# A two-layer graph network on one core: VectorE's work per supertile of the sort reduced or moved, node stages with two buffers, the first table split inside the gather pass

## The reference

```python
def reference(x, src, dst, edge_attr_4, W, ...):       # 12500 nodes, 412500 edges sorted by dst, D = 64
    h = relu(layernorm(x));  x = x + layer0(h, (src, dst), W)
    h = relu(layernorm(x));  x = x + layer1(h, (src, dst), edge_attr_4, ...)
    return x
def layer0(input, edge, weight):                        # hyperbolic attention
    h = mobius_matvec(weight, input, C)
    dist = sqdist(h[edge[0]], h[edge[1]], C)
    edge_e = exp(-leaky_relu(logmap0(C / (C + dist)), 0.2))
    h_prime = segment_sum(edge_e * logmap0(h)[edge[1]], edge[0])
    out = elu(h_prime / segment_sum(edge_e, edge[0]))
    return proj(expmap0(out, C), C)
def layer1(h, edge, edge_attr, ...):                    # message passing, four batch norms
    m = bn_relu(concat(h[src], h[dst], edge_attr) @ Wm1 + bm1)
    m = bn_relu(m @ Wm2 + bm2)
    u = bn_relu(concat(h, segment_sum(m, src)) @ Wu1 + bu1)
    return bn_relu(u @ Wu2 + bu2)
```

## Time and profile before

| what | value |
|---|---|
| median of 3 runs | 17072.78 us (17068.78 to 17084.48) |
| profiled execution, its own time | 17093.01 us |
| its span | 17091.3 us |
| busy: PE | 6354.3 us (37%) |
| busy: DVE | 8652.0 us (51%) |
| busy: ACT | 4054.6 us (24%) |
| busy: POOL | 9635.6 us (56%) |

### The profile page before, as it was taken

How to read it: one execution, slowest core, us unless ns; L and a number is a source line. 1 busy time by engine, 2 the same in 40 slices (tenths; PEclk the granted TensorE clock), 3 DMA queues, 4 the chain that set the end, 5 groups by cost and what they waited for, 6 DMA issues and landing times. The chain is left out here.

```text
span 17091.3 us, 195568 instructions
## 1 busy us (share of the span) xinstructions
PE 6354.3 (37%) x50077; PEld 5035.1 (29%) x50078; DVE 8652.0 (51%) x18303; ACT 4054.6 (24%) x7861; POOL 9635.6 (56%) x9968
## 2 busy tenths in 40 slices
PE   2444444311111111111159522323223223258996
PEld 2444444300000000000058511111111111125995
DVE  5888888623333333333268733333333333346884
ACT  1666666400000000000058400000000000024333
POOL 0555555466656665666657356666666666622773
PEclk7777777655555555555579756655655656579998
DMA  2000000133323332323444222222222222275331
GB/s 58 8 8 8 8 8 8 27 75 75 75 66 73 75 74 68 74 69 74 67 106 151 67 66 66 68 63 68 67 65 68 65 66 68 65 145 187 106 107 54
DMA packets 1142331, 1160.59 MB, mean 68 GB/s; under 512 B 688769, under 2 KB 832769, under 8 KB 1142018
## 3 DMA queue, kind: packets, MB, share of 16 engines
q1 hardware_dynamic: 845634, 680.39, 13.9%
q0 software_dynamic: 235008, 248.13, 8.6%
q10 hardware_dynamic: 61632, 231.44, 3.4%
HBM read 872.56 MB, written 286.75 MB: 68 GB/s over the span
## 5 line engine op out<-in xcount | busy, mean ns | idle before, releaser
L1559 POOL DMA_INDIRECT big<-b_d,big x3424 | 3284.0, 959 | 2270.7 <-POOLq L144 1232.2
L1084 POOL DMA_INDIRECT big<-h_d,big x3424 | 3273.9, 956 | 2001.9 <-issue 1189.0
L1145 DVE TENSOR_REDUCE ps<-ps 128x260 f32<-128x780 f32 x856 | 837.8, 979 | 3275.1 <-remote 1441.1
L1126 PE MATMUL ps<-big 128*128 x3424 | 737.9, 373 | 4609.0 <-issue 3388.5
L1686 DVE TENSOR_REDUCE ps<-ps 128x256 f32<-128x768 f32 x856 | 827.6, 967 | 2582.9 <-DVEq L144 1605.9
L1126 PEld LDWEIGHTS ps<-big 128*128 128x128 bf16 x3424 | 442.4, 162 | 4904.3 <-issue 4901.1
L1638 PE MATMUL ps<-big 128*128 x3424 | 608.7, 335 | 2615.9 <-issue 2130.1
L1885 POOL TENSOR_SCALAR big<-iota_f,big 128x128 f32<-128x128 f32 x1498 | 880.4, 608 | 827.7 <-DMA big<-rec_d 528.3
L1638 PEld LDWEIGHTS ps<-big 128*128 128x128 bf16 x3424 | 444.6, 160 | 2973.7 <-issue 2973.7
L777 ACT ACTIVATE big<-big 128x512 bf16<-128x512 bf16 x1736 | 1076.7, 708 | 907.1 <-ACTq L144 907.1
L1092 ACT ACTIVATE big<-big 128x16 int32<-128x16 f32 x214 | 49.1, 229 | 4899.9 <-issue 2304.5
(11 more groups left out here) (409 smaller groups left out, 14488.7 us busy)
## 6 DMA issues: line engine op xcount, KB each, us to landing
big<-e_d SPq DMA_DIRECT2D x428, 512.0 KB, 3.1
rows_d<-big ACTq DMA_DIRECT2D x214, 544.0 KB
big<-rows_d SPq DMA_DIRECT2D x214, 544.0 KB, 3.2
HA<-slots_d SPq DMA_DIRECT2D x214, 512.0 KB
big<-slots_d SPq DMA_DIRECT2D x214, 512.0 KB
e_d<-big ACTq DMA_DIRECT2D x214, 512.0 KB
big<-rec_d SPq DMA_DIRECT2D x860, 64.0 KB, 2.9
big<-h_d,big POOLq DMA_INDIRECT x3424
```

Of the source, the lines that this page charges most:

```text
L1084: gp.indirect_dma_start(G[g][:, t * ROW:(t + 1) * ROW], None, h0_d, bass.IndirectOffsetOnAxis(idx[g % 2][:, t:t + 1], 0)).then_inc(gath[g] ...
L1126: m = t.matmul(XS[q % 2][:, n, 0:3 * D + 3], OT3[g % 2][:, o, :], T0[:, ds(chunks[o // 2] * TW, 3 * D + 3)], start=True, stop=True)
L1145: v.tensor_reduce(xrow[:, q * QT:(q + 1) * QT, :], XS[q % 2][:, :, 0:3 * D + 3].rearrange("p t (q w) -> p t w q", q=3), AX, ALU.add).then_ ...
L1559: gp.indirect_dma_start(G[g][:, t * D:(t + 1) * D], None, b_d, bass.IndirectOffsetOnAxis(idx[g % 2][:, t:t + 1], 0)).then_inc(gath[g], 16)
```

## The change

**Blanks and edges.** `blank` gets a place of its own at the end of `big` and is set in the starting block; the fill of `rec_d` moves from the sort into SP's queue of the first node stage, which awaits it at its end; the weights for `wblk` go ahead of the edges.

```diff
             def _(sp):
+                sp.wait_ge(s_w, 1)
+                for h in range(2):
+                    sp.dma_start(wblk[h * D:(h + 1) * D, h * D:(h + 1) * D], w0t).then_inc(s_st, 16)
                 for t_, a_ in ((s_i, src), (d_i, dst)):
                     sp.dma_start(t_[0:P - 1, :], a_[0:(P - 1) * COLS].rearrange("(p j) -> p j", p=P - 1)).then_inc(s_edges, 16)
                     sp.dma_start(t_[P - 1:P, 0:LASTE], a_[(P - 1) * COLS:E].rearrange("(p j) -> p j", p=1)).then_inc(s_edges, 16)
-                sp.wait_ge(s_w, 1)
-                for h in range(2):
-                    sp.dma_start(wblk[h * D:(h + 1) * D, h * D:(h + 1) * D], w0t).then_inc(s_st, 16)
+                sp.dma_start(rec_d.rearrange("(k p t) w -> p k (t w)", p=P, t=TB),
+                             blank.unsqueeze(1).to_broadcast([P, NBLK + 2, TB * REC])).then_inc(s_blank, 16)
...
                 sp.wait_ge(s_v, 82)
                 sp.dma_start(h0_d.rearrange("(c p) w -> p c w", p=P), ROWS).then_inc(s_st, 16)
                 sp.wait_ge(s_st, 48)
                 sp.wait_ge(s_edges, 64)
+                sp.wait_ge(s_blank, 32)
```

**Node stages with two buffers.** In the first node stage, in layer 1's and in the final blocks the loops are unrolled; `hT`, `uT`, `stage` and, but for two cases, the PSUM areas exist twice; the node stages transpose straight from `HB` without a copy; PE puts the transpositions of round i+1 ahead of the product of round i. The first one's PE program (the others are alike):

```diff
                 t.wait_ge(s_st, 32)
-                with t.Fori(0, NIT) as i:
-                    hold(t, "t", g_in, i + 1)
+                t.wait_ge(s_v, 14)
+
+                def turn(i):
+                    if i >= 2:
+                        t.wait_ge(g_cp, i - 1)
...
+                turn(0)
+                for i in range(NIT):
+                    if i + 1 < NIT:
+                        turn(i + 1)
+                    product(i)
```

In layer 1's, ACT copies the second product from PSUM to `AG` and each round is stored on its own:

```diff
-                    link(v.tensor_copy(SB3, PAB[:, :, D:2 * D]))
-                    link(v.tensor_copy(AG[:, ds(i * W, W)], SB))
...
+                    a.activation(AG[:, i * W:(i + 1) * W].rearrange("p (c d) -> p c d", d=D), PAB[:, :, D:2 * D], ACT.Copy
+                                 ).then_inc(g_b, 1)
```

In the final blocks the PSUM areas alternate in the second and third (`h = i % 2 * 2048`) and stay single in the first. The addition of `AG` and `AG2`, one instruction ahead of the loop before, is made round by round, `bn_stats` follow round by round (`chunk_stats`), and the output is stored in 7 pieces and the last rows:

```diff
+        def chunk_stats(v, link, Y, i):
+
+            done = lambda n: min(n * W // NS5, 25)
+            for n in range(done(i), done(i + 1)):
+                ins = v.bn_stats(nst[:, n * 6:(n + 1) * 6], Y[:, n * NS5:(n + 1) * NS5])
...
+                concat(0)
+                concat(1)
                 link, k = chain(v, s_v)
-                node_stats(v, link, Y1, mv1, colp[:, 2:3], colp[:, 4:5], sc1, sh1, s_a, 1)
+                for i in range(NIT):
+                    if i + 2 < NIT:
+                        concat(i + 2)
+                    v.wait_ge(f_y, i + 1)
+                    chunk_stats(v, link, Y1, i)
+                node_stats(v, link, mv1, colp[:, 2:3], colp[:, 4:5], sc1, sh1, s_a, 1)
...
+                for i in range(NIT):
+                    sp.wait_ge(f_add, i + 1)
+                    c0, c1 = i * CPI, min((i + 1) * CPI, NCH - 1)
+                    sp.dma_start(out[c0 * P:c1 * P, :].rearrange("(c p) d -> p c d", p=P), X[:, c0:c1, :]).then_inc(s_out, 16)
```

```diff
-                        last = t.matmul(joint2, HI[b][:, m:NHI * w:step], LO[b][:, m:NLO * w:step], start=(n == 0 and m == 0),
+                        last = t.matmul(joint2, LO[b][:, m:NLO * w:step], HI[b][:, m:NHI * w:step], start=(n == 0 and m == 0),
```

```diff
-        ACTD = 14
+        ACTD = 16
...
-                    need(go(v.tensor_tensor(hit3, INC.unsqueeze(1).to_broadcast([P, NW, NC + 1]),
-                                            g8.unsqueeze(2).to_broadcast([P, NW, NC + 1]), ALU.is_le)))
-                    need(go(v.tensor_tensor(hit3, hit3, STEP.unsqueeze(1).to_broadcast([P, NW, NC + 1]), ALU.mult)))
-                    need(go(v.tensor_reduce(dsum, hit3, AX, ALU.add)))
+                    for w in range(NW):
+                        n = go(v.scalar_tensor_tensor(out=hit3[:, w, :], in0=INC, scalar=g8[:, w:w + 1], in1=STEP,
+                                                      op0=ALU.is_le, op1=ALU.mult, accum_out=dsum[:, w:w + 1]))
+                    need(n)
...
+                def attributes(b):
+
+                    consume(gp, att_in[b], 32)
+                    a3 = attb[b].rearrange("p (j a) -> p j a", a=4)
+                    r3 = rem.rearrange("p (j a) -> p j a", a=4)
+                    gp.tensor_copy(PA[b][:, :, 0, :], a3).then_inc(s_piece, 1)
+                    gp.wait_ge(s_piece, 1)
+                    gp.tensor_tensor(r3, a3, PA[b][:, :, 0, :], ALU.subtract).then_inc(s_piece, 1)
...
                 def spread(b, s):
+                    attributes(b)
                     consume(gp, l_rdy)
-                    consume(gp, pa_rdy)
```

```diff
+                sp.dma_start(R0, h0_d.rearrange("(c p) w -> p c w", p=P)).then_inc(s_table, 16)
...
+                t.wait_ge(t0_rdy, 1)
                 each_block(t, step)
...
+                v.wait_ge(s_table, 16)
+                piece3(v, split, R0[:, :, 0:D], R0t, T0q)
+                piece3(v, split, R0[:, :, SQ:SQ + 1], q2t, T2q)
+                v.sem_inc(t0_rdy, 1)
```

363 lines of the change are left out of this document (198 added, 165 removed).

## The result

| | before | after |
|---|---|---|
| median of 4 runs each | 17070.78 us | 16429.32 us |
| lowest and highest | 17068.22 to 17084.48 | 16424.54 to 16432.72 |
| span of the profiled execution | 17091.3 us | 16422.8 us |

The ratio is 0.9622 (95% interval 0.9606 to 0.9639): 641 us or 3.8% less.

What follows compares the result with a forecast made beforehand. Each stage between barriers has its own limit, DVE in the supertiles; 76 + 8 + 295 + 40 + 3 + 72 + 100 = 594 us off the profiled 17093.0 gives 16499, as a median 16480, range 16370 to 16640.

Steps and rivals of the forecast that it cites:

- First node stage: Node stage before the sort: weights first start PE 78 us sooner; stage ends at 212, saving 76 us, bounds 60 and 100.
- Histogram: Sort's histogram with swapped operands: gain up to 38 us or loss of 15 possible, costed at nothing.
- Wait for the casts: DVE's wait for `s_cast` before the first `flags` in the sort goes: 8 us saved.
- Supertiles: Sort's supertiles: DVE saves 3.0 us each, period falls from 23.2 to 20.8, 295 us saved; bounds 370 and 135.
- the second loop: Supertiles' chain through POOL's `spread` and PE's `place` and `ranks`: 20.6 us, 20.8 with a hand-over, becomes the bound.
- the rival to which I gave 0.15: Supertiles: chain over POOL and PE is shorter, or histogram gains clock; period 20.2, 75 us better, 16405; chance 0.15.
- POOL and DVE hinder each other: Supertiles: POOL's new instructions each stall DVE 0.36 us; DVE at 22.1, 135 us saved instead of 295, 16640; chance 0.15.
- First table: First table's load and split beside the first gathers: 52 us of stage go, 12 given back, 40 saved, bounds 30 and 52.
- Middle stage: Middle stage: one instruction over 6272 elements, 3.43 us, goes; 3 us saved.
- Node stage of layer 1: Seven rounds of 17.2 us fall to 8.0 with two buffers; 72 us saved in all, bounds 65 and 80.
- Final blocks: Three final blocks: `bn_stats` taken round by round and two buffers; 20, 42 and 38, together 100 us, bounds 80 and 115.
- Slower: Supertiles: POOL's five instructions take 2.3 us or more each; at 2.5 the time is about 17215; chance 0.02.

Runs made afterwards that it cites:

- the first eight experiments: Seven kernels with parts of the change undone, added to or alone, and one with the fill behind the store, on two other chips: 14675.8 to 14999.3 us.

## Why the prediction was right, point by point

- **First node stage** (76 forecast, 71.5 measured). Weights ahead of the edges and PE's start near 74 came out, and so did the end inside 190 to 225. The row of edges, fill and store that I added up to 221 was nearer than the overlapping fill that I leaned to with 212. Two things stood against the overlap. SP was held in issuing the edges until 115, which the earlier trace rows show in the weights' issue at 114.89, so the fill could not start before. And the edges' engine isn't free of the fill: over 128 partitions it takes all 16 engines by the section of the Trainium skill that I quoted (*DMA: Bandwidth & Descriptors*, "Why a DMA increments its semaphore by 16 and not by 1"). The trace agrees: the share is 1.00 until 166, and one engine works on until 190, since its part of the fill stays behind the edges. Splitting the edge loads showed it (187.5).
- **Histogram** (nothing, nothing). 403 products take 76.3 us in both orders of the operands, at the clock of 0.50 in both; neither bound, +38 or -15, came near. No row stood behind the 15, and nothing here shows why the two shapes cost the same.
- **Wait for the casts** (8, 8.0).
- **Supertiles** (295, 337.5). DVE's saving of 3.0 us was 2.75: attributes 1.45 for 1.56, one-hots 0.67 for 0.65, `hit3` 0.59 for 0.78, by the three experiments that undo each. The step that was off is the second loop: "20.6 us after 1515.79", with a hand-over 20.8. That was one supertile, and a long one: the mean is 20.4, and 20.1 in the changed kernel. The hand-over is 0.15 us. So PE's loop stands at about 20.3 in the mean, just under DVE's 20.45, and DVE stays the bound. That is the rival to which I gave 0.15, and its outcome is the right one, 20.45 between my 20.8 and its 20.2; but its reasons are not shown: `place` starts only 0.1 us sooner (8.2 us into the supertile after 8.3), and PE's own stretch is nearly as long as before. That the period landed between the two has luck in it: DVE saved 0.25 us less than forecast, and the loop that I took for the bound is half a microsecond shorter than I priced it, 20.3 for 20.8. The mean granted clock over 400 to 2700 us does rise as the period falls (0.72 at 23.13, 0.73 at 21.87, 0.74 at 21.09 and 21.01, 0.75 at 20.58 and 20.42), but that is the shorter period alone: with levels of 0.50 and 1.00 each of these is 10.1 to 10.3 us at the higher level in a supertile.
- **POOL and DVE hinder each other** (rival, 0.15). Its 1.9 us are refuted in the sort, by attributes back on DVE and by eight more instructions on POOL; 0.24 us of it are real.
- **First table** (40, 36). The 12 us that I set aside for POOL's waits at the buffers were 15, but for another reason: three gathers held up by DVE's split. There the contention that I had placed in the sort costs the most.
- **Middle stage** (3, 3.4). From its first DVE instruction to the node stage it takes 106.9 us before and 103.5 after.
- **Node stage of layer 1** (72, 91). Mis-sized: I had PE's 7.1 us a round as fixed and added a hand-over, 8.0 in all; the round is 5.62 us, at a clock of 0.87 instead of 0.58 (two rounds are shown below). PE's 14 products take 3.26 us in it instead of 5.57: 2.3 us a round, an estimate of 16 of the 19 us that the forecast lacks. Nor was PE the longer engine, as I wrote: DVE's 53.0 us are more than PE's 49.8.
- **Final blocks** (100, 110.7). With the first product of the second and third as the marks between them, the first block saved 19.7 us (forecast 20), the second 49.7 (42), the third 41.2 (38). PE's clock is 0.78, 0.89 and 0.81 in them, where the kernel before had 0.81, 0.66 and 0.55: the two whose clock rose are the two that saved more. That fits the cause of the node stage; no experiment parts it from the rest.
- **Slower** (rival, 0.02). POOL's five instructions took 0.27 to 0.37 us, not 2.3; the price worked out from L810 and L812 was right to 0.1.

Two rounds of the node stage of layer 1 in the changed kernel (L1467 opens DVE's part of a round, L1504 are PE's products):

```profile
9253.34 1.09 DVE L1467 TENSOR_TENSOR big<-ps,big 128x896 f32<-128x896 f32 x1 [0.18 <-PE ps L1504]
9254.52 0.92 ACT L1483 ACTIVATE HA<-ps 128x896 f32<-128x896 f32 x1 [3.89 <-DVEq L1468]
...
9255.59 3.26 PE L1504 MATMUL ps<-big 128*128 128x256 f32 x14 [1.59 <-ACT HA L1483]
...
9258.96 1.09 DVE L1467 TENSOR_TENSOR big<-ps,big 128x896 f32<-128x896 f32 x1 [0.18 <-PE ps L1504]
```

From 9253.34 to 9258.96 is the round: DVE's L1467, ACT's copy of the second product out of the same PSUM area (L1483), PE's 14 products, one behind the other, 1.09 + 0.92 + 3.26 us and 0.35 of hand-overs. The seven stores (L1454, SP busy with them from 9249.85 on) lie beside the rounds.

What stays open: what PE's gaps without a releaser are and why two of the chips have none; why the positions on DVE take 0.10 us less beside POOL's attributes; and what makes the gather passes differ by up to 45 us between executions of the same kernel and by 830 to 930 between chips.

## What to carry to other kernels

A loop that isn't the bound today is read over many rounds before it is priced as the next bound: here one supertile said 20.6 and later another 18.7, and the means are 20.4 and 20.1. Where a change makes PE's work denser in a stage whose granted clock was low, its products are priced at both levels of the clock. Before small instructions go to POOL, see beside which DVE instructions they will fall. Before a large transfer is moved to another place in a queue, ask which DMA engines the transfers ahead of it use and how long the issuing engine itself is held, and not only what waits for its end. Undoing one part at a time, read by the distance between two marks of the trace, gives values to some 5 us of 2500 where the whole time of the kernel varies by up to 40 on one chip.

## What the runs showed of the hardware

- A gather issued by POOL (0.94 us) that met a DVE subtraction with two inputs in SBUF, or a cast that moved 6336 elements in 3.50 us, lasted until 0.7 to 0.8 us behind it (3.75, 6.56, 7.04 us). Casts of 6.76 us on the same number of elements delayed none.
- DVE instructions beside POOL's: the fourth L689 (two inputs, 100 elements) took 0.53 us beside a POOL subtraction of 0.37, and 0.32 otherwise; an L664 that met POOL's 4.40 us instruction took 2.40 us instead of 0.20.
- SP was held 72 us (118.62 to 190.7) in issuing a transfer of 128 KB behind one of 13824 KB, and 47 us in another order; it was held 58.61 us in issuing the one-partition part of an edge load behind the 127-partition one.
- A load of 127 partitions moved 26 GB/s; the same edges in 112 and 15 partitions, with the fill beside them, went at 320 GB/s.
- Four DVE instructions with an accumulated output on 100 elements have a pitch of 0.24 us, though each is 0.32 long.
- PE's granted clock was 0.58 over the node stage of layer 1 with rounds of 17 us and PE idle for two thirds of the stage, and 0.87 with rounds of 5.6; 26 products of `place` took 2.80 us at 0.50 (1.2 GHz) and 1.53 at 1.00 (2.4 GHz).
- PE had gaps without a releaser inside `place` on the chips of the first and the last runs (59 us in the supertiles before, 91 with 17 one-hots), and none on the two chips of the first eight experiments.
